# Two sums for the scatter-added expert results instead of three, in a mixture-of-experts layer on one core

## What is computed

```
x = layernorm(x + attention(x))                      # x1: 4096 rows of 256
probs = softmax(x1 @ gate_w.T);  top 6 of probs + gate_b;  cw = chosen probs
y = sum over e of cw[:, e] * ((silu(x1 @ w1[e].T + b1[e]) * (x1 @ w3[e].T + b3[e])) @ w2[e].T + b2[e])
z = (silu(x1 @ ws1.T + bs1) * (x1 @ ws3.T + bs3)) @ ws2.T + bs2
out = layernorm(x1 + y + z)
```

## Time and profile before

| | |
|---|---|
| median of 3 runs | 1085.8 us (1080.98 to 1086.66) |
| span of the profiled execution | 1081.8 us |
| busy share of the span | PE 92%, PEld 73%, DVE 75%, ACT 68%, POOL 70% |
| DMA moved | 176.26 MB, mean 163 GB/s |
| scatter-adds | 207, 69 into each of three tensors |

### The profile page before, as it was taken

How to read it: one execution, slowest core, us unless ns; L and a number is a source line. 1 busy time by engine, 2 the same in 40 slices (tenths; PEclk the granted TensorE clock), 3 DMA queues, 4 the chain that set the end, 5 groups by cost and what they waited for, 6 DMA issues and landing times.

```text
span 1081.8 us, 27903 instructions
## 1 busy us (share of the span) xinstructions
PE 992.7 (92%) x7478; PEld 790.0 (73%) x7479; DVE 810.6 (75%) x2622; ACT 733.6 (68%) x1859; POOL 752.6 (70%) x677
## 2 busy tenths in 40 slices
PE   8999999999999997888799999999999999999872
PEld 4546555555565654458798899999999999999872
DVE  8786878788888887747866677777777777777596
ACT  4567676666766665656455688878888888888545
POOL 4234458788888888777653677777777777777576
PEclk9899999999999999869899999999999999999985
DMA  6634254555555555457688888888887888888793
GB/s 186 175 104 118 73 155 138 181 156 179 164 172 171 167 153 189 144 171 236 204 252 220 207 137 132 132 133 131 132 130 129 137 132 132 132 134 178 190 382 128
DMA packets 134404, 176.26 MB, mean 163 GB/s; under 512 B 19328, under 2 KB 111536, under 8 KB 134064
## 3 DMA queue, kind: packets, MB, share of 16 engines
q1 hardware_dynamic: 88016, 105.83, 33.0%
q0 software_dynamic: 39024, 54.29, 29.2%
q10 hardware_dynamic: 7280, 15.11, 4.5%
HBM read 73.68 MB, written 78.17 MB: 140 GB/s over the span
## 4 chain that ended last, share of the span: by engine, by line
PE 67%; DVE 15%; ACT 6%; issue 5%; DMA 3%; POOL 2%; ACTq 1%; SPq 0%; POOLq 0%; DVEq 0%
PE psum L1099 17%; PE psum L828 10%; PE psum L1126 6%; PE psum L873 6%; PE psum L861 5%; DVE rowmax L1602 4%; PE psum L1129 4%; PE psum L842 4%; PE psum L1082 4%; PE psum L1112 2%; ACT probs L1222 2%; PE psum L1113 2%; PE psum L848 1%; DMA z_d<-y_sb,tokens 1%; DVE x1p L1618 1%
## 5 line engine op out<-in xcount | busy, mean ns | idle before, releaser
L1222 ACT ACTIVATE probs<-psum 128x512 f32<-128x512 f32 (+2 forms) x384 | 186.4, 530 | 117.5 <-PE psum L861 115.5
L1602 DVE TENSOR_REDUCE rowmax<-psum 128x1 f32<-128x512 f32 (+3 forms) x352 | 211.9, 632 | 55.6 <-PE psum L848 53.0
L2157 POOL DMA_INDIRECT xs_d<-x1p,index x192 | 204.4, 1065 | 57.8 <-issue 40.3
L1099 PE MATMUL psum<-we_hi_lo,xb_hi 128*128 x828 | 207.1, 332 | 0.0
L2229 POOL DMA_INDIRECT x_d<-y_sb,tokens x69 | 108.5, 1572 | 54.8 <-issue 31.7
L1952 DVE TENSOR_TENSOR hb<-psum,hb 128x176 f32<-128x176 f32 x207 | 70.6, 341 | 101.4 <-ACT hb L1399 97.8
L2069 POOL TENSOR_SCALAR_AFFINE_SELECT probs<-probs 128x512 f32<-128x512 f32 x128 | 88.1, 689 | 78.7 <-ACT probs L1222 76.5
L1099 PEld LDWEIGHTS psum<-we_hi_lo,xb_hi 128*128 128x128 f32 x828 | 136.9, 188 | 3.1 <-issue 0.2
L842 PE MATMUL psum<-stack_k,stack_q 96*128 96x256 bf16 (+3 forms) x512 | 129.4, 311 | 8.0 <-DVE rowmax L1602 3.4
L2229 POOL DMA_INDIRECT z_d<-y_sb,tokens x69 | 107.9, 1563 | 38.9 <-issue 25.7
L861 PE MATMUL psum<-stack_q,stack_k 99*128 99x256 bf16 (+3 forms) x512 | 119.2, 308 | 17.1 <-ACT probs L1222 14.8
(11 more groups left out here) (227 smaller groups left out, 2537.3 us busy)
## 6 DMA issues: line engine op xcount, KB each, us to landing
xb<-xs_d SPq DMA_DIRECT2D x207, 138.0 KB
stack_q<-q_h SPq DMA_DIRECT2D x48, 128.0 KB
stack_k<-k_h SPq DMA_DIRECT2D x45, 128.0 KB
w_raw<-in_we SPq DMA_DIRECT2D x9, 608.0 KB
xT_raw<-in_xT SPq DMA_DIRECT2D x9, 512.0 KB, 4.6
stack_q<-q_m SPq DMA_DIRECT2D x32, 128.0 KB
stack_k<-k_m SPq DMA_DIRECT2D x32, 128.0 KB
x_res<-in_x SPq DMA_DIRECT2D x8, 512.0 KB, 4.2
```

What stands on the lines that cost most here:

```text
L1099: last = nc.tensor.matmul(uv, (xb_hi, xb_lo)[a][k % 2][:, d, :], w_flat[:, bass.ds(at + b * W_COLS + d * UP, UP)], start=False, stop=d == ...
L1222: nc.scalar.activation(probs[kt][:, heads[0]:heads[0] + n, :], st[f % ST_BANKS][:, 0:n * width].rearrange("p (h t) -> p h t", h=n), ACT.Ex ...
L1602: nc.vector.reduce_max(rowmax[gpar][:, heads[0]:heads[0] + n, qt], src, AX.X).then_inc(sm_free, 1)
L2157: nc.gpsimd.indirect_dma_start(out=xs_d[:, :], out_offset=bass.IndirectOffsetOnAxis(ap=index[tp][:, n:n + 1], axis=0), in_=x1p[tp][:, n // ...
```

## The change

SUMS goes from 3 to 2: block k's add goes to `x1_d` for even k and to `z_d` for odd k, and waits for the add two blocks back. `y_d`, its zeroing, its final loads, DVE's third adds and their buffers `fin_y` go. `load_first_chunk` no longer waits for the zeroing, but for two DMAs that SP issued before the first batch and that read the same block of constants. `x1T_late` (the inputs of the late chunks) is placed right behind `x1T_end`, ahead of `fin_x`, where the weights of a lower expert were; its loads are issued as before. `added` and `adds_by_turns` follow SUMS (16 x 12 / 2 increments a turn).

```
-SUMS = 3
+SUMS = 2
-Y_PIECES = B - 1
-Y_ROWS = P * -(-(T_ALL + P) // (P * Y_PIECES))
...
-        y_d = nc.dram_tensor("y_d", (T_ALL + P, D), fp32).ap()
...
         X1T_END = [X1T[0], sb("x1T_end", [P, 2, KD, HT_TOK], f32r)]
+        x1T_late = [sb(f"x1T_late{n}", [P, KD, HT_TOK]) for n in range(HALVES - HC1 - 1)]
         fin_x = [sb(f"fin_x{n}", [P, HALF, D]) for n in range(HALVES)]
         fin_z = [sb(f"fin_z{n}", [P, HALF, D]) for n in range(HALVES)]
-        fin_y = [sb(f"fin_y{n}", [P, HALF, D]) for n in range(HALVES)]
-        x1T_late = [sb(f"x1T_late{n}", [P, KD, HT_TOK]) for n in range(HALVES - HC1 - 1)]
...
-            def set_third_sum(piece):
-                rows = y_d[Y_ROWS * piece:min(Y_ROWS * piece + Y_ROWS, T_ALL + P)]
-                sp.dma_start(rows.rearrange("(q p) d -> p q d", p=P),
-                             pad_block[:, 0:D].unsqueeze(1).to_broadcast([P, rows.shape[0] // P, D])).then_inc(y_set, 16)
...
-                if b < Y_PIECES:
-                    set_third_sum(b)
                 load_shift(4 * b + 3, par, 1, 3)
...
-                sp.wait_ge(y_set, 16 * Y_PIECES)
+                sp.wait_ge(pad_stored, 16)
+                sp.wait_ge(pads_set, 16)
...
-            for n, src, dst in ((0, x1_d, fin_x), (1, z_d, fin_z), (2, y_d, fin_y)):
+            for n, src, dst in ((0, x1_d, fin_x), (1, z_d, fin_z)):
                 sp.wait_ge(added[n], 16 * ((BLOCKS + SUMS - 1 - n) // SUMS))
                 for i in FINAL_ORDER[:FINAL_FIRST]:
                     load_final(i, src, dst)
             for i in FINAL_ORDER[FINAL_FIRST:]:
                 load_final(i, x1_d, fin_x)
                 load_final(i, z_d, fin_z)
-                load_final(i, y_d, fin_y)
...
                 dve.wait_ge(fin_sum, m + 1)
-                dve.wait_ge(fin_third_loaded[i], 16)
-                nc.vector.tensor_tensor(fin_x[i][:], fin_x[i][:], fin_y[i][:], ALU.add).then_inc(fin_third, 1)
-                dve.wait_ge(fin_third, m + 1)
...
-                else:
-                    pool.wait_ge(y_set, 16 * Y_PIECES)
                 settle(pool, passed_pool)
                 nc.gpsimd.indirect_dma_start(
-                    out=(x1_d, z_d, y_d)[k % SUMS][:, :], out_offset=bass.IndirectOffsetOnAxis(ap=tokens[:, k:k + 1], axis=0),
+                    out=(x1_d, z_d)[k % SUMS][:, :], out_offset=bass.IndirectOffsetOnAxis(ap=tokens[:, k:k + 1], axis=0),
```

More of the change, by code:

```diff
@@ L515, in postln_layer @@
         added = [sem(f"added{n}") for n in range(SUMS)]
-        y_set = sem("y_set")
         seeded = sem("seeded")
@@ L523, in postln_layer @@
         fin_loaded = [sem(f"fin_loaded{n}") for n in range(HALVES)]
-        fin_third_loaded = [sem(f"fin_third_loaded{n}") for n in range(HALVES)]
         fin_sum = sem("fin_sum")
-        fin_third = sem("fin_third")
         fin_stats_done = sem("fin_stats_done")
@@ L763, in load_final @@
             def load_final(i, src, dst):
-                sp.dma_start(dst[i][:], rows_of(src, i)).then_inc((fin_third_loaded if src is y_d else fin_loaded)[i], 16)
+                sp.dma_start(dst[i][:], rows_of(src, i)).then_inc(fin_loaded[i], 16)
             def store_final(k):
```

## The result

The changed kernel takes 1134.3 us (median) against 1084.1 us before: ratio 1.0477, with a 95% interval of 1.0442 to 1.0512. The forecast was 1137 us. One of the changed kernel's four executions took 1360.2 us at a mean granted clock of 0.65, where the others had 0.97, and is not in the ratio; the median of the other three is 1134.1 us. The profiled execution of the changed kernel has a span of 1132.6 us, 50.8 us over the 1081.8 of before.

A forecast was written before the change was run, and what follows sets the result against it. PE's pace bounds the block stage before; with two sums POOL's serial adds would. Block stage +60 us (44 + 9 + 7), end stage starting 57 later, end -6: span 1132.8, plus 4.0 to the median, 1137 us; range 1105 to 1165.

The forecast's parts named there:

- The deciding step: Block stage: adds in a sum are serial, so two sums make POOL's adds the bound, 2.325 us a block against PE's 2.06.
- C: Time from an add's issue start to the next one's in the same sum, if nothing else holds it; taken as 4.65 us.
- The far row: Last scatter into xs_d, a POOL DMA before the block stage, read as an upper bound of C = 5.51 us.
- The price of the quiet stretch: Block stage, 166 blocks from 640.42 to 982.62 us: 2.325 instead of 2.061 us a block, +44 us.
- The first rival: Block stage: adds land sooner with fewer bytes in flight, C = 4.22, 2.11 us a block, 1092 us; chance 0.10.
- The rival of stronger contention: Block stage: block loads of xb may always meet the adds' packets, C = 5.1, 1182 us; chance 0.13.
- C < 4.12: Block stage: adds stay hidden in the quiet stretch and PE stays the bound, 1079 us; chance 0.05.
- The first blocks: First 26 blocks, beside large weight and bias loads: slower pace plus slow cycles costing a block each, +9 us.
- The last blocks: Last 15 blocks, 982.62 to 1012.67 us: slower pace plus one slow cycle by the end's loads, +7 us.
- The start of the end stage: From last add to DVE's shared-result add: final loads wait for the last add; stage begins 57 us later, not 60.
- The end: Final stage: DVE's third add goes, 7.85 us of the chain with 1.75 already counted, -6 us.
- Edits at nothing: Zeroing DMAs removed (gain 0, at most 3 us), replaced wait in load_first_chunk, fin_y loads removed, x1T_late moved: 0 each.

The follow-up runs named there:

- The wait alone: Kernel before, three sums and all their work kept, but POOL's add of block k also waits for the add of block k-2 to land: 1145.0 us, ratio 1.0599.

## Why the prediction was right, point by point

Before and after by stages, in their two profiles:

| stage | before, us | after, us | change | forecast |
|---|---|---|---|---|
| to the first add | 578.9 | 575.3 | -3.7 | 0 |
| first 26 blocks | 61.5 | 74.9 | +13.4 | +9 |
| quiet stretch, 166 blocks | 342.2 | 391.7 | +49.5 | +44 |
| last 14 intervals to the last add | 30.0 | 34.1 | +4.1 | +7 |
| last add to the first shared-result add | 14.9 | 9.3 | -5.6 | -3 |
| from there to the end | 54.3 | 47.4 | -6.9 | -6 |
| span | 1081.8 | 1132.6 | +50.8 | +51 |

The span came out within 0.2 us of the forecast, and that closeness is luck: stages missed by +9.9 us (first blocks, quiet stretch) and by -10.1 us (the rest) cancel. What held is the mechanism and its size.

- *The deciding step held.* C = 4.65 was chosen, 4.72 measured on average (4.65 to 4.72 over the kernels with two sums, 2.327 to 2.360 a block), with a median of 4.58. The wait alone gives the whole loss, one sum doubles it. The far row, 5.51 us from the lone scatter, misled in its size: in the chain above the changed kernel's adds land 3.74 to 3.86 us after their start. The Trainium skill (DMA: Bandwidth & Descriptors, on the anatomy of a SWDGE DMA) gives its fit, 2.0 us plus bytes over 436 GB/s, for a whole DMA with its setup. My estimate of 4.66 us set those 2.3 us behind the 1.56 us of issue, which the page does not say. Read my way this trace agrees (these adds land 2.2 to 2.3 us after the issue ends); read as the page has it, it would give an estimate of C = 2.3 + 0.8 = 3.1 us, and the trace does not agree. (The far row's side sum was also off: worked as the rest is, it comes to about +148 us and not +143.)
- *The price of the quiet stretch* was 5.5 us low, and the tail of long cycles is why, since the typical cycle of 4.58 lies under the 4.65 taken. Some 5 us of it is the slow cycle shown above: the adds at 1028.98 and 1036.28 are 7.3 us apart instead of 2.3. I had booked it under the last blocks, where the same loads made it before (issued from 977.32 on); with slower blocks they came inside this stretch. The first rival (C = 4.22 by lighter load) fell: with one sum the DMA share is half that of two, and it took 0.16 us off the average cycle, a third of what that rival needed, and 0.04 off the median. The Trainium skill's rule that a lighter HBM load shortens a DMA's fixed cost (DMA: Bandwidth & Descriptors, latency and other measured facts) is right in direction, and small here by those numbers. The rival of stronger contention (5.1) fell too, and C < 4.12 with it.
- *The first blocks* cost 4.4 us more than worked out. I let each slow cycle cost one block at the quiet pace; I counted three, and the changed kernel has four in a row, of 6.9 to 8.9 us, eight blocks in 30.1 us. POOL's adds into x there (each with one into z between them):

```profile
585.77 1.56 POOL L2210 DMA_INDIRECT x_d<-y_sb,tokens  x1 [1.29 <-ACT y_sb L1404]
...
594.62 1.56 POOL L2210 DMA_INDIRECT x_d<-y_sb,tokens  x1 [0.30 <-issue]
...
601.61 1.56 POOL L2210 DMA_INDIRECT x_d<-y_sb,tokens  x1 [0.30 <-issue]
...
608.93 1.56 POOL L2210 DMA_INDIRECT x_d<-y_sb,tokens  x1 [0.30 <-issue]
...
615.87 2.12 POOL L2210 DMA_INDIRECT x_d<-y_sb,tokens  x1 [0.30 <-issue]
```

  Most of the miss is in the other 18 blocks: they take 44.75 us, 2.49 each and not 2.325, which makes 2.9 of the 4.4 us. The fourth slow cycle has a likely reason in the traces, which was not tried on its own. ACT issues the bulk loads by block number; before, those at 601.77 and 604.91 were 3.1 us apart, and the last slow cycle began between them; in the changed kernel, with its slower blocks, the ones that answer to them, at 600.85 and 607.01, were 6.2 us apart, and behind each a slow cycle began, at 601.61 and at 608.93. This term was mis-sized by half.
- *The last blocks* cost 3 us less. There was a slip in my count: from the add at 982.62 to the last one are 14 intervals, not 15, and 14 x 2.325 = 32.6 gives +2.5. And the slow cycle that I put here at +2.3 ran earlier, in the quiet stretch. The other 1.6 us of the measured +4.1 lie in the last two intervals, 2.85 and 3.55 us, behind the loads of x1T_late that SP issued from 1067.43 on.
- *The start of the end stage.* The sign was right, the landing time wrong. I took 5.3 us for the first loads, and the first z load landed in 3.3; it was also issued 4.6 us after the last add's start, and not the 5.25 of the working. The chain of the changed kernel there:

```profile
1080.55 3.31 DMA fin_z<-z_d
1083.86 0.07 issue
1083.93 1.27 POOL fin_x L2221
1085.22 0.70 DVE fin_x L1972
```

  It is not the missing third load that does it: with the wait alone, and all three sums loaded, the gap from the last add to that point is 9.5 us too (1077.44 to 1086.97). The adds lag behind PE, so x1T_late's loads lie earlier: SP issued them from 1067.43 on, 8.5 us ahead of the last add, and before from 1010.74 on, 1.9 us ahead of it. That this made the landing shorter was not tried on its own.
- *The end.* 7.85 us on the chain less 1.75, so -6, measured -6.9. The chain's share was a good price; with PE's pace kept the same stretch fell by 7.4 and 8.8 us (third sum left out, third sum loaded but not added). POOL was indeed next late: its final sums, h_lo and rstd now lead with ACT's normalization.
- *Edits at nothing.* The zeroing was priced right. The first add did start at 575.3, before the 576 that I had named as a sign against this, but with the zeroing back it starts at 574.9. The x1T_late move and the changed wait were not tried on their own; no stage of the table needs them.
- *The offset.* I added 4.0 us to get from the span to the median. Of the changed kernel's median only 1.7 lies above its profiled span; the rest of the 4.0 belonged to that one execution of before, and that is 2.3 of the 2.7 us by which the total was high.
- *What I said the profile would show* was wrong in two places. As POOL's releaser I expected the add's DMA, and it says ACT's y_sb. And PE's busy share did not fall to 88% but to 96%; its matmul count did the falling, to 89%.

## What to carry to other kernels

When a step must wait for its predecessor's landing, count the whole round, issue, landing and wake, and divide by the number of independent targets; compare that with the pace of the engine that now binds, and a target too few turns the round into the pace. A round that nothing waits for today can't be read from one row, but its packets bound it from below and any waiter on a like transfer from above, and the waiter closest in kind, not the loneliest, is the one to trust. When the releaser that a profile names ended much closer to the start than that pair of engines ever manages, look for another event at the same time.

## What I had not expected of the hardware

In these runs the landing of such an add depended little on load while no bulk transfer ran: the median cycle was 4.54 us at a DMA share of 0.38 and 4.58 at 0.73, while beside bulk loads it reached 8.83 and 9.16. So a few long cycles, not the typical one, made the differences in pace between kernels with two sums. And the time to the first add varied by 4.8 us (574.15 to 578.94) over profiles of kernels whose work up to there is the same but for the zeroing.
